# Where the second layer rounds its attention output between two batches: on VectorE in pairs, with GpSimd and the first exponentials no longer held back

## What is computed

```python
def act_quant(x):
    s = 127.0 / jnp.clip(jnp.max(jnp.abs(x), axis=-1, keepdims=True), EPS)
    xq = jnp.clip(jnp.round(x * s), -128, 127) / s
    return x + lax.stop_gradient(xq - x)
...
xn = adaln(x, c, g1, w_ada1, b_ada1)
qkv = bitlinear(xn, w_qkv, b_qkv).reshape(B, T, 3, H, hd)
q, k, v = (qkv[:, :, i].transpose(0, 2, 1, 3) for i in range(3))
attn = jax.nn.softmax(jnp.einsum('bhqd,bhkd->bhqk', q, k) * hd ** (-0.5), axis=-1)
o = jnp.einsum('bhqk,bhkd->bhqd', attn, v).transpose(0, 2, 1, 3).reshape(B, T, D)
x = x + bitlinear(o, w_proj, b_proj)
```

## Time and profile before

| | |
|---|---|
| median of three runs | 2775.66 us (2775.62 to 2777.38) |
| profiled execution, its own time | 2772.19 us |
| its span | 2770.4 us |
| PE busy | 2607.1 us, 94% |
| DVE busy | 2149.7 us, 78% |
| POOL busy | 1963.1 us, 71% |
| ACT busy | 1841.1 us, 66% |
| granted TensorE clock, mean | 0.984 |

### The profile page before, as it was taken

One profiled execution on the slowest core, in us unless ns is written; L12 is line 12 of the kernel. 1 busy time (PEld: TensorE's weight loads), 2 busy tenths in 40 slices (PEclk: granted clock), 3 DMA queues, 4 the chain that ended last, 5 costly groups with the idle time before them and its releaser, 6 DMA issues. The chain is left out here.

```text
span 2770.4 us, 59968 instructions
## 1 busy us (share of the span) xinstructions
PE 2607.1 (94%) x21716; PEld 1458.3 (53%) x21761; DVE 2149.7 (78%) x4440; ACT 1841.1 (66%) x3320; POOL 1963.1 (71%) x1579
## 2 busy tenths in 40 slices
PE   7899999999999999999769998999899999987997
PEld 5655566555665547555335554555455445543443
DVE  5777778776787768877667778777877787768997
ACT  4366665666566675566556677667766776667996
POOL 0298844897359872789749887987789778965542
PEclk9999999999999999999989999999999999999999
DMA  6122353224432335223223214321332232245444
GB/s 236 39 59 59 113 169 108 59 59 150 143 96 61 88 111 173 72 58 101 85 73 82 59 33 119 82 59 29 110 82 59 46 106 59 59 164 182 104 103 110
DMA packets 168764, 260.42 MB, mean 94 GB/s; under 512 B 85388, under 2 KB 91668, under 8 KB 167576
## 3 DMA queue, kind: packets, MB, share of 16 engines
q1 hardware_dynamic: 166680, 250.27, 33.0%
q0 software_dynamic: 1792, 6.33, 0.6%
HBM read 99.15 MB, written 38.88 MB: 50 GB/s over the span
## 5 line engine op out<-in xcount | busy, mean ns | idle before, releaser
L547 DVE TENSOR_REDUCE a_mxs<-ps 128x1 f32<-128x512 f32 x2048 | 1267.8, 680 | 258.8 <-PE ps L414 256.2
L508 ACT ACTIVATE a_p<-ps 128x512 f32<-128x512 f32 x2048 | 1043.6, 605 | 203.3 <-PE ps L428 193.1
L368 POOL TENSOR_TENSOR a_sum<-a_p 128x512 f32<-128x512 f32 x736 | 940.0, 1287 | 201.8 <-PE ps L448 112.8
L414 PE MATMUL ps<-a_k,a_q 96*128 96x512 f32 x2048 | 854.6, 424 | 25.8 <-DVE a_mxs L547 20.8
L428 PE MATMUL ps<-a_q,a_k 98*128 98x512 f32 x2048 | 807.3, 419 | 15.6 <-ACT a_p L508 9.8
L448 PE MATMUL ps<-a_sum,a_unit 128*32 128x512 f32 x1536 | 650.5, 596 | 0.6 <-POOL a_sum L368 0.6
L374 POOL TENSOR_TENSOR a_sum<-a_sum,a_p 128x512 f32<-128x512 f32 x480 | 619.3, 1290 | 37.6
L448 PE MATMUL ps<-a_p,xv 128*32 128x512 f32 x3968 | 638.9, 595 | 0.0
L414 PEld LDWEIGHTS ps<-a_k,a_q 96*128 96x128 f32 x2048 | 388.7, 190 | 258.5 <-DVE a_mxs L547 104.9
L428 PEld LDWEIGHTS ps<-a_q,a_k 98*128 98x128 f32 x2048 | 383.9, 189 | 243.3 <-ACT a_p L508 144.9
L517 ACT ACTIVATE a_ots<-ps 128x512 f32<-128x512 f32 x256 | 152.8, 598 | 402.7 <-PE ps L448 401.6
(11 more groups left out here) (253 smaller groups left out, 3080.6 us busy)
## 6 DMA issues: line engine op xcount, KB each, us to landing
a_q<-qh SPq DMA_DIRECT2D x256, 128.0 KB, 2.3
a_k<-kh SPq DMA_DIRECT2D x256, 128.0 KB, 2.4
a_q<-ql SPq DMA_DIRECT2D x128, 128.0 KB, 2.3
a_k<-kl SPq DMA_DIRECT2D x128, 128.0 KB, 2.4
x<-a_p SPq DMA_DIRECT2D x64, 256.0 KB, 2.2
a_p<-in_w_fc SPq DMA_DIRECT2D x12, 1024.0 KB, 7.9
kh<-in_x SPq DMA_DIRECT2D x4, 2048.0 KB, 14.5
a_p<-x SPq DMA_DIRECT2D x16, 512.0 KB, 5.8
```

The costliest lines, as they stand in the source:

```text
L368: pair = pool.tensor_tensor(tile, keys[0], keys[1], ALU.add)
L414: pe.matmul(self.mx[self.mx_ring[at]], self.q[j][0:96, t * P:(t + 1) * P], self.k[j][0:96, half * HALF:(half + 1) * HALF], start=True, sto ...
L508: act.activation(self.key_tile(u, kt), self.st[self.st_ring[CHUNKS * k + n]], ACT.Exp, scale=self.scale).then_inc(self.s_exp, 1)
L547: dve.reduce_max(self.mxs[:, k % 2, c:c + 1], self.mx[self.mx_ring[CHUNKS * k + c]], axis=AX.X).then_inc(self.s_mxr, 1)
```

## The change

The eight `eight_bits` of a passage now stand two by two: 0 and 1 behind QK10, 2 and 3 behind V5, 4 and 5 behind V6, 6 and 7 behind V7, each pair ahead of that product's two maxima. POOL no longer waits for `s_q` in any passage nor in the last `work`; it does the value biases of tiles 3 and 4 at once, then the eight residual additions, and the value biases of tiles 5 to 7 behind these. The first exponentials wait for the unit whose tile they overwrite, one by one. In `TAIL_ONLY` the order on DVE stays as it was.

```diff
-    def run_act(self, act, b, extra=None, upper=None):
+    def run_act(self, act, b, extra=None, upper=None, lower=None):
...
                     for r in range(2):
+                        if k == 0 and s < 4 and lower:
+                            lower(2 * s + r)
                         self.exp(act, k, N, self.pair(b, i, k - 1), s, r)
...
+        BITS = {("QK", EARLY + 2): (0, 1), ("V", LEAD): (2, 3), ("V", LEAD + 1): (4, 5), ("V", LEAD + 2): (6, 7)}
...
                     if nxt is not None:
-                        biases(range(EARLY_V))
-                    pool.wait_ge(s_q, TT * (tail + 1))
-                    if nxt is not None:
-                        biases(range(EARLY_V, TT))
+                        biases(range(LEAD))
                     pool.wait_ge(s_late, 16 * (tail + 1))
                     for t in range(TT):
                         if t % 2 == 0:
                             pool.wait_ge(s_res[t // 2], 16 * (tail + 1))
                         pool.tensor_tensor(xres[:, t, :], xres[:, t, :], bp, ALU.add).then_inc(s_xb, 1)
                     if nxt is not None:
+                        biases(range(LEAD, TT))
                         for v in range(EARLY, UN):
                             rest(v)
...
-                    act.wait_ge(s_lo, UN * (b + 1))
-                    att.run_act(act, b, extra, upper=lambda: act.wait_ge(s_store, 16 * TT * b + 16))
+                    att.run_act(act, b, extra, upper=lambda: act.wait_ge(s_store, 16 * TT * b + 16),
+                                lower=lambda n: act.wait_ge(s_lo, UN * b + EARLY + n + 1))
...
-                        if (kind, n) == ("QK", EARLY + 2) and tail is not None:
-                            for t in range(TT):
+                        if tail is not None and nxt is not None:
+                            for t in BITS.get((kind, n), ()):
                                 eight_bits(tail, t)
```

## The result

The changed kernel takes **2800.14 us** (median of 6 runs, 2796.82 to 2804.1), the kernel before 2776.03 us on the same chip (6 runs, 2774.42 to 2777.54): 1.0087 times as long, 95% interval 1.0077 to 1.0098, so 24.1 us slower. 2789.5 had been forecast, with 2797 as the upper end: the sign was right, the size too small by 10.6.

The account below looks back on a forecast made before the run. The prediction took DVE to pace each passage, with PE busy 94% of the span. Passages +9.6, last batch +5.7 and first exponentials -1.4 made 13.9 us on 2775.66, so 2789.5 us, range 2780 to 2797.

Parts of the forecast that it names:

- POOL's lost cover: Without POOL's wait, its additions and DVE's roundings exclude each other and take turns, 0.90 us more for each rounding.
- The turn of 1.42 us: A DVE rounding that follows another with POOL queued takes 1.42 us end to end, against 0.52 apart before.
- The passages, +9.6: Three passages, first rounding to QK11: 3 x 0.99 us later plus six lost ties at 1.10 us, +9.6 us.
- The tie of 0.03 us: DVE's rounding 2 and POOL's next addition start 0.03 us apart, nine times in all; POOL expected to win six.
- rival 3: PE's clock stays at its lower level beyond QK11: 2.8 us a passage, 8.4 in all, 2797.9 us; chance 0.05.
- Behind the last batch, +5.7: Behind the last batch, roundings colliding with POOL's additions end at 2489.6 instead of 2483.84, delaying transposes and projection: +5.7 us.
- The first exponentials, -1.4: At the start of batch 0, ACT no longer waits 1.37 us for POOL's last low part: -1.4 us.
- The sum: Whole kernel: +9.6 + 5.7 - 1.4 = 13.9 us slower, 2789.5 us.
- Rival 1: Roundings and POOL's additions do not exclude each other: 9.2 us faster, 2766.4 us; chance 0.12.
- what the pairs alone would bring: In each passage, without collisions, paired roundings bring QK11 2.65 us earlier; 7.8 us for three passages.
- Rival 2: Residual loads land after 1682, so roundings 0 and 1 run free: +2.7 us, 2778.4 us; chance 0.08.

Follow-up runs that it names:

- experiments 6 and 8: 6: changed kernel, its eight roundings also writing an accumulator, 2784.53 us; 8: changed kernel, POOL waiting for the scales and for all eight roundings, 2766.19 us.
- Experiment 7: Changed kernel with the eight roundings and the three 128x8 scale operations also writing an accumulator: 2776.27 us.
- before_new_pool: Kernel before, roundings together, with the changed kernel's POOL program (no wait, residual additions ahead of value biases 5 to 7): 2803.74 us.
- exps_alone: Kernel before with only the early exponentials each waiting for their own tile: 2775.66 us.
- Experiment 10: Two kernels: the kernel before plus the exponentials' own waits (exps_alone), 2775.66 us; both_waits with the exponentials waiting for all low parts again, 2773.03 us.
- both_waits: Changed kernel with POOL waiting for the scales before value biases 3 and 4, and for all eight roundings before the residual additions: 2766.19 us.
- wait_in_tail: Changed kernel with POOL's wait for all eight roundings put back behind the last batch alone: 2797.35 us.
- before_free_pool: Kernel before with only POOL's wait for the roundings taken away, its old order of additions kept: 2785.24 us.

## Why the prediction was right in sign and too small

- **POOL's lost cover.** Right. An instruction of the same form elsewhere in the kernel gave the mechanism; the roundings went from 427 to a median of 1299 ns, and experiments 6 and 8 show from two sides that the additions are the cause. The turn of 1.42 us holds too: behind the last batch, while POOL has additions left, the roundings start 1.41 us apart.
- **The passages, +9.6.** This is the step that failed: three of them cost 18.7. From the first rounding to QK11 it is 3.05 us more, against 0.99 to 4.3 forecast with 3.2 as the mean; that part was sized right, though in part by luck. The tie of 0.03 us came in the first stage of each passage, and POOL won all three (roundings of 1.52 us). The other six ties did not come: POOL was at value biases by then, which wait for ACT's V5 and V7, and had started 0.68 and 0.53 us ahead of the rounding, which makes 0.87 and 1.02 us instead of 1.53. The term lacked the 3.10 us in A. I had written POOL's value bias of tile 4 and the first residual additions into 1678 to 1682 and DVE's first rounding at 1681.20, and never asked what DVE does in between: it makes the scales, by three operations of the same kind as the roundings, 0.17 to 0.18 us each and so below any attention, but each pays for a whole addition of POOL. Experiment 7 gives back exactly these 3.1 us. The last 0.66 stands in C, which begins at 1703.01 with PE's clock still at its lower level (0.50 from 1702 to 1706): a beginning of rival 3, a quarter of its 2.8. In before_new_pool, where C begins at 1705.67 and the clock reads 1.00 from 1704 on, it is missing (22.68).
- **Behind the last batch, +5.7.** Scales (1.9) and roundings (4.4) make 6.2 in the trace: nearly right in size, by another make-up, since the scales were missed here too and the roundings' share was 1.3 too large: POOL was out of additions before the last two roundings, not only before the last. The 2.7 us of S are apart from it (below).
- **The first exponentials, -1.4.** The wait for POOL is gone, and against ACT's instructions 40 us earlier the first exponential comes 1.0 us sooner (0.8 to 1.8 in the kernels with this edit, not at all in the three without). By the fifteenth exponential 1.2 are lost again: PE's granted clock is 0.64 from 1448 to 1456, where before it was 0.94.

```profile
1448.00:1456.00 8.00, 8.00 (x27) 5.71 (x29) 6.67 (x14) 6.38 (x13) 6.39 (x6) 0.64 0.06 13
```

  That loss is not this edit's: the three experiments without it lose 0.6 to 1.5 over the same exponentials, exps_alone nothing. Experiment 10 finds nothing for the edit in the medians, so whether a part of the 1.4 arrives is open. I had priced a start and not an arrival.
- **The sum.** In the traces 18.7 + 6.2 + 2.7 us make 27.6 of the 28.1 that are left without the 3.8 at 1406 us; the medians say 24.1. So some 4 us of the traces' difference are not there in a usual run, and the terms above hold for the traces.
- **The rivals.** Rival 1 was the size of the gain without collisions, 2766.4 us: both_waits, in which nothing collides, takes 2766.19. So the working of "what the pairs alone would bring" (2.65 a passage and 1.4) was sound in size, with the make-up off: 3.1 a passage, and the exponentials' share in the passages rather than at batch 0, where the prediction gave it nothing. That the two totals meet to 0.2 us is luck. Rival 2 did not come: POOL ran on without a gap. The collisions in A, 9.3 for three passages, added to the forecast's 2789.5 give 2798.8, 1.3 below what was measured.

Open is S. After the change PE makes the last projection in 9.44 us, in wait_in_tail, where nothing around it differs from before, in 8.80, and in exps_alone and both_waits in 6.85. In the windows after, the clock comes back from its lower level (1.2 GHz of 2.4) only behind 2520:

```profile
2516.00:2520.00 4.00, 2.78 (x7) 1.05 (x8) 0.75 (x1) 1.17 (x3) 0.00 (x0) 0.50 0.02 4
2520.00:2524.00 4.00, 4.00 (x15) 1.63 (x14) 2.25 (x3) 2.08 (x6) 0.00 (x0) 0.74 0.36 136
```

In both_waits S is 1.6 us longer than before although its projection is not: there PE's first fifteen 128x512 matmuls of the second half take 6.55 us instead of 4.93, with the clock at 0.63 from 2504 to 2508. Ten kernels have an S between 30.4 and 31.7, three one of 28.8 to 29.1. These three (before, before_free_pool, exps_alone) are the ones that keep in the passages both the row of eight roundings and POOL's old order of additions; why that should reach to here, or whether it is chance in one trace each, I have not tested.

## What to carry to other kernels

When a wait of one engine is removed, list every instruction of the other engines that falls into the stretch it had kept free, down to the 0.17 us ones: a small operation that is shut out for the length of a large one costs as much as a large one does. Here the wait was worth keeping, and its place was worth moving: put the work that is free to run in the gaps, the wait right before the operations that collide, and what nobody needs soon behind what somebody waits for (2766.19 against 2776.04 and 2800.14 us). And a single edit has no price of its own: the exponentials' own waits were worth nothing that the medians show in one order of POOL's work and some 4 to 7 us in another (in C 0.0 and 1.7 us a passage).

## What the runs showed of the hardware

- A TENSOR_SCALAR of 128x8 elements in SBUF takes 0.17 to 0.18 us alone and 1.0 to 1.28 us beside a row of POOL's 128x512 additions: the price of the collision is set by POOL's instruction, not by DVE's.
- The same rounding with an accumulator takes 0.685 us plus 0.083 for reading it, beside POOL or not, against 0.427 alone and 1.30 (median) beside POOL. One that costs 0.26 us more when nothing runs beside it (0.34 with the reading) was 15.6 us cheaper for the kernel when something does.
- TENSOR_REDUCE from PSUM, TENSOR_TENSOR from PSUM and SBUF, and RECIPROCAL of 128x8 (0.20 us) kept their length beside the same additions (1.27 for two maxima throughout).
